# Ten of a group's 36 probability tiles turned through memory in place of seven, kept weights in 2 KB packets, new instruction orders

## The reference

```python
def attention(x):                       # on layernorm(x)
    q = rmsnorm((x @ Wq.T) per head, q_norm_w)      # 32 heads of 128
    k = rmsnorm((x @ Wk.T) per head, k_norm_w)      # 8 heads of 128
    v = x @ Wv.T                                    # 8 heads of 128
    scores = q @ k.T / sqrt(128)                    # 4 query heads share one k/v head
    bias = where(rel > 0, -1e30, slope[head] * rel) # causal, rel = key - query
    return (softmax(scores + bias) @ v) @ Wo.T
def lora(x):                            # on layernorm(x)
    gates = 8 * softmax(x @ Wr.T + br)              # 8 experts of rank 16
    return 2 * sum over h of gates[h] * (x @ A[h].T) @ B[h].T
x = x + attention(layernorm(x)); x = x + lora(layernorm(x))
```

## Time and profile before

| | |
|---|---|
| median of 3 runs | 2136.99 us (2133.37 to 2137.82) |
| the profiled execution's own time | 2138.16 us |
| its span, first to last instruction | 2136.3 us |
| granted TensorE clock, mean | 0.993 |
| instructions | 33509 |
| busy share: PE, DVE, ACT, POOL | 98%, 63%, 54%, 44% |
| DMA | 329095 packets, 176.81 MB, of which 243800 packets under 512 bytes |

### The profile page before, as it was taken

One profiled execution on the slowest core, in us unless ns is written; L12 is line 12 of the kernel. 1 busy time (PEld: TensorE's weight loads), 2 busy tenths in 40 slices (PEclk: granted clock), 3 DMA queues, 4 the chain that ended last, 5 costly groups with the idle time before them and its releaser, 6 DMA issues.

```text
span 2136.3 us, 33509 instructions
## 1 busy us (share of the span) xinstructions
PE 2083.0 (98%) x11772; PEld 1786.4 (84%) x11772; DVE 1355.6 (63%) x3431; ACT 1148.2 (54%) x3314; POOL 936.1 (44%) x984
## 2 busy tenths in 40 slices
PE   7999999999999999999999999999999999999997
PEld 6888888888888888888888888888888888888885
DVE  6656656566565665658876556566566656656676
ACT  4555545555454654645445555555555555555552
POOL 3443434444444443444443544435453443545443
PEclk9999999999999999999999999999999999999998
DMA  4152141511415125051350422313041231304112
GB/s 158 64 140 75 30 130 64 154 60 40 133 54 150 60 55 157 16 154 55 110 157 7 113 70 68 101 50 92 28 107 62 67 102 50 89 30 106 44 36 73
DMA packets 329095, 176.81 MB, mean 83 GB/s; under 512 B 243800, under 2 KB 301144, under 8 KB 320736
## 3 DMA queue, kind: packets, MB, share of 16 engines
q1 hardware_dynamic: 305264, 72.41, 15.3%
q10 hardware_dynamic: 23664, 102.25, 12.8%
HBM read 99.11 MB, written 75.50 MB: 82 GB/s over the span
## 4 chain that ended last, share of the span: by engine, by line
PE 83%; DVE 4%; issue 4%; DMA 3%; SPq 2%; POOL 2%; ACT 2%; ACTq 0%; DVEq 0%; POOLq 0%
PE s_ps L1026 17%; PE q_ps L1026 15%; PE y_ps L1026 15%; PE o_ps L1026 15%; PE turn_ps L1113 13%; PE turn_ps L1026 5%; DMA p_raw<-p_bounce 3%; SPq L568 2%; POOL probs_odd L799 1%; PE turn_ps L1107 1%; PE y_ps L1186 1%; DVE pT_lo L898 1%; DMA p_bounce<-probs_odd 1%; DVE y L955 0%; DVE oT_lo L949 0%
## 5 line engine op out<-in xcount | busy, mean ns | idle before, releaser
L799 POOL TENSOR_TENSOR probs_odd<-probs_odd,p_inv 128x256 f32<-128x256 f32 (+3 forms) x256 | 316.4, 1256 | 326.9 <-DVE p_inv L928 326.9
L706 ACT ACTIVATE pT_hi<-turn_ps 128x512 fp32r<-128x512 f32 x464 | 271.6, 597 | 316.2 <-PE turn_ps L1113 315.9
L799 POOL TENSOR_TENSOR probs_even<-probs_even,p_inv 128x128 f32<-128x128 f32 (+3 forms) x256 | 261.8, 1044 | 386.1 <-DVE p_inv L928 386.1
L898 DVE TENSOR_TENSOR pT_lo<-turn_ps,pT_hi 128x512 fp32r<-128x512 f32 x464 | 314.6, 684 | 146.2 <-ACT pT_hi L706 145.2
L921 DVE CUSTOM_DVE_ANT_0 probs_odd<-s_ps,rel 128x256 f32<-128x256 f32 (+3 forms) x256 | 209.3, 820 | 131.9 <-issue 131.4
L1026 PE MATMUL s_ps<-kT_hi,qT_hi 128*128 128x512 f32 (+3 forms) x768 | 278.7, 363 | 2.6 <-DVE kT_lo L900 1.8
L1026 PE MATMUL s_ps<-kT_hi,qT_lo 128*128 128x512 f32 (+3 forms) x768 | 262.9, 342 | 0.0
L1026 PE MATMUL s_ps<-kT_lo,qT_hi 128*128 128x512 f32 (+3 forms) x768 | 262.1, 341 | 0.0
L720 ACT ACTIVATE probs_odd<-probs_odd,neg_max 128x256 f32<-128x256 f32 (+3 forms) x256 | 211.9, 832 | 76.0 <-DVE neg_max L921 75.9
L921 DVE CUSTOM_DVE_ANT_0 probs_even<-s_ps,rel 128x128 f32<-128x128 f32 (+3 forms) x256 | 174.0, 686 | 118.0 <-issue 117.2
L1026 PE MATMUL o_ps<-pT_hi,v_hi 128*128 128x512 f32 x576 | 243.9, 423 | 1.9 <-DVE pT_lo L898 0.9
(11 more groups left out here) (110 smaller groups left out, 4578.6 us busy)
## 6 DMA issues: line engine op xcount, KB each, us to landing
p_raw<-p_bounce SPq DMA_DIRECT2D x448, 64.0 KB, 2.3
p_bounce<-probs_odd SPq DMA_DIRECT2D x64, 256.0 KB, 2.3
wq_kept<-wqT_hi ACTq DMA_DIRECT2D x8, 1024.0 KB, 5.8
wq_kept<-wqT_lo ACTq DMA_DIRECT2D x8, 1024.0 KB, 8.4
wo_kept<-woT_hi ACTq DMA_DIRECT2D x8, 1024.0 KB, 8.1
wo_kept<-woT_lo ACTq DMA_DIRECT2D x8, 1024.0 KB, 10.2
p_bounce<-probs_even SPq DMA_DIRECT2D x64, 128.0 KB, 1.8
wqT_hi<-wq_kept ACTq DMA_DIRECT2D x8, 1024.0 KB, 4.8
```

The costliest lines, as they stand in the source:

```text
L706: nc.scalar.activation(target, bank, ACT.Copy).then_inc(sems["high"], 1)
L799: nc.gpsimd.tensor_tensor(row, row, p_inv[:, s % 2, h:h + 1].to_broadcast((P, L)), ALU.mult).then_inc(sems["normalise"], 1)
L898: nc.vector.tensor_tensor(target, bank, upper.bitcast(F32), ALU.subtract).then_inc(sems["low"], 1)
```

## The change

Three things are edited. The table gets three more tiles: (4,4), (5,4) and (6,4), so 10 of 36 go through memory. The kept weights get another layout in HBM, with one piece of 512 floats for each partition after the other, so that a packet has 2 KB where it had 4 KB (wkv) or 8 KB (wq, wo). And all the lists are written anew; GROUP_A is shown in part.

```diff
-MEMORY_TILES = {5: (5,), 6: (5, 6), 7: (4, 5, 6, 7)}
+MEMORY_TILES = {4: (4,), 5: (4, 5), 6: (4, 5, 6), 7: (4, 5, 6, 7)}
 GROUP_A = (
...
-    "high.p.6.0 o_low.5 fetch_p.6.5 high.p.6.1 low.p.6.0 exp.7.2 low.p.6.1 send_p.7.1 fetch_p.6.6 scores.7.3 "
...
+    "fetch_p.6.4 square_q.8 low.p.6.0 load_wkv y.5 inv_q.8 max.7.2 exp.7.1 high.p.6.1 invert.7.0 normalise.7.0 "
+    "exp.7.2 scores.7.3 low.p.6.1 values.6.0 max.7.3 normalise.7.1 send_p.7.0 values.6.1 fetch_p.6.5 turn.p.6.2 "
+    "add_y.5 exp.7.3 turn.kv.0 norm_q.8 high.p.6.2 fetch_p.6.6 invert.7.1 flip_p.6.4 normalise.7.2 low.p.6.2 "
+    "upper_p.6.4 send_p.7.1 turn.p.6.3 high.kv.0 normalise.7.3 send_p.7.2 turn.kv.1 keep_wq low.kv.0 high.p.6.3 "
+    "lower_p.6.4 send_p.7.3 low.p.6.3 flip_p.6.5 values.6.2 flip_p.6.6 upper_p.6.5 values.6.3 high.kv.1 lower_p.6.5 "
+    "values.6.4 fetch_p.7.4 low.kv.1 q.9.0 upper_p.6.6 turn.p.7.0 lower_p.6.6 q.9.1 fetch_p.7.5 high.p.7.0 turn.q.8 "
+    "low.p.7.0 values.6.5 high.q.8 values.6.6 fetch_p.7.6 low.q.8 turn.p.7.1 o_high.6 turn.kv.2 load_wo o_low.6 "
+    "high.p.7.1 flip_p.7.4 low.p.7.1 upper_p.7.4 lower_p.7.4 values.7.0 high.kv.2 values.7.1 fetch_p.7.7 low.kv.2 "
...
-        wkv_kept = nc.dram_tensor("wkv_kept", [NG, 2, P, C * 2 * HD], F32).ap()
-        wq_kept = nc.dram_tensor("wq_kept", [NG, 2, P, C * W512], F32).ap()
-        wo_kept = nc.dram_tensor("wo_kept", [NG, 2, P, G * DM], F32).ap()
+        wkv_kept = nc.dram_tensor("wkv_kept", [NG, 2, C // 2, P, W512], F32).ap()
+        wq_kept = nc.dram_tensor("wq_kept", [NG, 2, C, P, W512], F32).ap()
+        wo_kept = nc.dram_tensor("wo_kept", [NG, 2, G, P, DM], F32).ap()
+
+        def pieces(kept, g, part):
+            return kept[g, part].rearrange("c p n -> p c n")
+
+        def pairs(turned):
+            return turned[:].rearrange("p (a c) n -> p a (c n)", c=2).bitcast(F32)
...
-                act.dma_start(wq_kept[w + 1, 0], wqT_hi[:].rearrange("p c n -> p (c n)").bitcast(F32)).then_inc(wq_spilled, 16)
+                act.dma_start(pieces(wq_kept, w + 1, 0), wqT_hi[:].bitcast(F32)).then_inc(wq_spilled, 16)
...
-                act.dma_start(wqT_hi[:].rearrange("p c n -> p (c n)").bitcast(F32), wq_kept[g, 0]).then_inc(wq_back, 16)
+                act.dma_start(wqT_hi[:].bitcast(F32), pieces(wq_kept, g, 0)).then_inc(wq_back, 16)
```

More of the change, by code:

```diff
@@ L630, in keep_wkv @@
                 after(act, "low", "wkv", w + 1, 1)
-                act.dma_start(wkv_kept[w + 1, 0], wkvT_hi[:].rearrange("p c n -> p (c n)").bitcast(F32)).then_inc(wkv_spilled, 16)
-                act.dma_start(wkv_kept[w + 1, 1], wkvT_lo[:].rearrange("p c n -> p (c n)").bitcast(F32)).then_inc(wkv_spilled, 16)
+                act.dma_start(pieces(wkv_kept, w + 1, 0), pairs(wkvT_hi)).then_inc(wkv_spilled, 16)
+                act.dma_start(pieces(wkv_kept, w + 1, 1), pairs(wkvT_lo)).then_inc(wkv_spilled, 16)
             def keep_wq(w):
                 after(act, "low", "wq", w + 1, C - 1)
-                act.dma_start(wq_kept[w + 1, 0], wqT_hi[:].rearrange("p c n -> p (c n)").bitcast(F32)).then_inc(wq_spilled, 16)
-                act.dma_start(wq_kept[w + 1, 1], wqT_lo[:].rearrange("p c n -> p (c n)").bitcast(F32)).then_inc(wq_spilled, 16)
+                act.dma_start(pieces(wq_kept, w + 1, 0), wqT_hi[:].bitcast(F32)).then_inc(wq_spilled, 16)
+                act.dma_start(pieces(wq_kept, w + 1, 1), wqT_lo[:].bitcast(F32)).then_inc(wq_spilled, 16)
             def keep_wo(w):
                 after(act, "low", "wo", w, G - 1)
-                act.dma_start(wo_kept[w, 0], woT_hi[:].rearrange("p c n -> p (c n)").bitcast(F32)).then_inc(wo_spilled, 16)
-                act.dma_start(wo_kept[w, 1], woT_lo[:].rearrange("p c n -> p (c n)").bitcast(F32)).then_inc(wo_spilled, 16)
+                act.dma_start(pieces(wo_kept, w, 0), woT_hi[:].bitcast(F32)).then_inc(wo_spilled, 16)
+                act.dma_start(pieces(wo_kept, w, 1), woT_lo[:].bitcast(F32)).then_inc(wo_spilled, 16)
             def back_wkv(w):
@@ L647, in back_wkv @@
                 act.wait_ge(wkv_spilled, 32 * NG)
-                act.dma_start(wkvT_hi[:].rearrange("p c n -> p (c n)").bitcast(F32), wkv_kept[g, 0]).then_inc(wkv_back, 16)
-                act.dma_start(wkvT_lo[:].rearrange("p c n -> p (c n)").bitcast(F32), wkv_kept[g, 1]).then_inc(wkv_back, 16)
+                act.dma_start(pairs(wkvT_hi), pieces(wkv_kept, g, 0)).then_inc(wkv_back, 16)
+                act.dma_start(pairs(wkvT_lo), pieces(wkv_kept, g, 1)).then_inc(wkv_back, 16)
             def back_wq(w):
@@ L654, in back_wq @@
                 act.wait_ge(wq_spilled, 32 * NG)
-                act.dma_start(wqT_hi[:].rearrange("p c n -> p (c n)").bitcast(F32), wq_kept[g, 0]).then_inc(wq_back, 16)
-                act.dma_start(wqT_lo[:].rearrange("p c n -> p (c n)").bitcast(F32), wq_kept[g, 1]).then_inc(wq_back, 16)
+                act.dma_start(wqT_hi[:].bitcast(F32), pieces(wq_kept, g, 0)).then_inc(wq_back, 16)
+                act.dma_start(wqT_lo[:].bitcast(F32), pieces(wq_kept, g, 1)).then_inc(wq_back, 16)
             def back_wo(w):
@@ L661, in back_wo @@
                 act.wait_ge(wo_spilled, 32 * NG)
-                act.dma_start(woT_hi[:].rearrange("p c n -> p (c n)").bitcast(F32), wo_kept[g, 0]).then_inc(wo_back, 16)
-                act.dma_start(woT_lo[:].rearrange("p c n -> p (c n)").bitcast(F32), wo_kept[g, 1]).then_inc(wo_back, 16)
+                act.dma_start(woT_hi[:].bitcast(F32), pieces(wo_kept, g, 0)).then_inc(wo_back, 16)
+                act.dma_start(woT_lo[:].bitcast(F32), pieces(wo_kept, g, 1)).then_inc(wo_back, 16)
             def high(w, of, *which):
```

## The result

The changed kernel takes **2154.02 us** in the median of 4 runs (2153.06 to 2155.26), beside 2137.40 us for the kernel before on the same chip. The ratio is 1.0075, 95% interval 1.0062 to 1.0088: 0.75% slower, where the prediction had 1.5% faster. Its profiled execution took 2153.44 us, with a span of 2151.6 us and a mean granted clock of 0.989.

The account below looks back on a forecast made before the run. PE, busy 98%, was taken as the bound: 2138.2 - 20.6 - 16.6 + 7.0 - 6.8 + 3.2 + 2.0 = 2106.4 us profiled, 1.2 above the median of runs, so 2105 us predicted, range 2091 to 2122.

Parts of the forecast that it names:

- The turns: 48 tiles over 16 groups no longer turned by PE, at some 0.43 us a tile: 20.6 us off PE.
- So the wait at y goes: Groups 0 to 6: y's addition ahead of the last flips and transfers moved remove PE's seven y waits, 16.6 us gained.
- I take 1.0 us of wait in each of 7 groups: Value product 7.1 waits for its lower half behind the flip of 7.4: 7.0 us back.
- one for one: Packets of the two DMA queues pass about equally at either size, giving the fetch 3.5 times its rate beside kept weights.
- My bound of 2.9 us: Upper bound per group for the new wait at tile 7.1, today's longest; the lower bound was 0.
- The clock drops: Four falls to 1.2 GHz behind y waits of 1.9 to 2.95 us, none expected at 1.0: 6.8 us gained.
- 2 KB packets: Kept weights' smaller packets would free SP's issues; by the skill page's rule of whole bundles, the edit would be worth nothing.
- Short waits: New slips on PE, such as three s=6 tiles sharing two memory slots, 0.2 us a group: 3.2 us lost.
- The last group: Chain from tile 7's last normalising to product 7.7 has less PE work to hide it: 2.0 us lost, bounds 0 and 3.
- Two of the signs: Wrong if POOL lower-half waits exceed 0.5 us a group, flips wait 3 us with PE behind, or first-batch clock drops.
- the fetched tiles come too late: Slower rival: ten tiles, three raw buffers and POOL's work delay value products in all 16 groups, 2167 us; chance 0.04.

Follow-up runs that it names:

- e6: Kernel before, seven tiles and own lists, with only the keeping of wq moved behind the group's last upper_p in groups 0 to 6: 2109.48 us, ratio 0.9867.
- e1: Changed kernel with only the keeping of wq moved behind the last fetched tile's high half in groups 0 to 6: 2108.92 us, ratio 0.9868 to before.
- e13: Kernel before with only the addition of y for token tile 5 moved ahead of the flip of 7.5, groups 0 to 6: 2140.36 us, ratio 1.0009.
- e5: Changed kernel with both the keeping of wq and the load of Wo moved behind the last upper_p, groups 0 to 6: 2106.27 us, ratio 0.9854.
- e9: Changed kernel with wq's keeping and Wo's load late, but groups 7 and 15 with seven tiles and the lists of the kernel before: 2100.48 us, ratio 0.9827.
- e3: Changed kernel with the kept weights' old layout (8 KB pieces, wkv 4 KB), all lists and tiles as changed: 2151.86 us, ratio 1.0069 to before.
- e4: Kernel before with the kept weights' new layout alone (2 KB packets): 2140.58 us, ratio 1.0017.
- e8: Changed kernel with wq's keeping late, plus q.9.3 moved in groups 9 to 14 and token tile 6's gated-layer turns later in the last group: 2108.05 us.
- e11: Changed kernel with the keeping of wq moved earlier, directly behind low.wq.3 and beside that of wkv: 2108.22 us, ratio 0.9863 to before.
- e12: Changed kernel with only the lower half of wq (1 MB) kept late, behind the last upper_p: 2130.03 us, ratio 0.9971 to before.

## Why the prediction was wrong

The sum came to -31.8 us; the trace has +15.3. By stretches the 47 us are: groups 0 to 6 forecast -24.0, measured +9.6; group 7 -1.1 and +0.9; groups 8 to 14 -7.7 and -2.1; group 15 +0.9 and +6.2; ahead of group 0, 0 and +0.6.

- **The turns, -20.6 us: nearly right.** e6 against e1 gives 1.3 us for three tiles, 0.42 a tile as forecast, in groups 0 to 6, where nothing else stands. In the second batch PE's busy time falls by 1.1, 0.36 a tile, and the time by 0.2 to 0.3.
- **"So the wait at y goes", -16.6 us: right in the trace, wrong as a gain.** I took the place of the addition for the cause. e13 moved it alone and gained nothing; e6 left it alone, moved the transfer and gained 28 us, waits and clock drops together. The prediction had named the late fetch as the reason, and then booked the wait as if it hung on the order of DVE's queue.
- **"I take 1.0 us of wait in each of 7 groups": the step that failed.** The place was right, the size was 4.1 to 5.2 us, 31.8 us in all where 7.0 were booked. I counted wq's transfer against the fetch (3 us left of 5.4) and wrote that the send "adds a little since it too shares the engines". It is the send that falls into the transfer: 8.1 us to landing where e1 has 3.0. The load of Wo stands right ahead of the fetch, which I had noted in the list and not priced: 4.7 us to landing for 2.3. I had read the fetch beside that load as one for one, from 281.5 to 283.5 us of the kernel before. That stretch has wq's first packets in its second half; from 281.3 to 282.3, beside the load alone, 52 packets of the fetch pass while 135 of the load do. My bound of 2.9 us was the longest wait of the kernel before, and that is no bound for a chain in which three transfers now meet.
- **The clock drops, -6.8 us: wrong with it.** The waits of 4 us and more brought a low clock in every one of groups 0 to 6, in all 30.6 us at the lower level. Before it was 17: 13.6 in the four drops that the prediction counted and 3.4 at the head of group 0. At half of that time lost, as the prediction priced it, that is some 7 us more lost where 6.8 were to be gained. With the waits gone (e1, e5, e6, e9) there is none between 50 and 2070 us.
- **2 KB packets: nothing, as forecast.** e3 and e4 show no gain. SP's issues were not freed either: the longest of a fetch takes 2.9 us in e4 for 2.7 before. By the Trainium skill ("DMA: Bandwidth & Descriptors", Queues, rings and completion order) a bundle of descriptors passes before the engine turns to the other ring. That four small pieces then go as one large one was my own step; the page counts in descriptors. The counts of 348 to 332 at 2 KB and 99 to 61 at 8 KB fit single packets as well as equal bundles, and no run here shows a bundle.
- **Short waits, 3.2 us: too small.** In groups 9 to 14 it is 0.8 us each where 0.2 were booked: y.7 0.54 us behind the low half of o, and a value product 0.3 behind POOL's lower half. Each of the two is small; together they eat two thirds or more of what the three tiles give.
- **The last group, +2.0 us: too small.** With the turns and the short waits the forecast was +0.9, measured +6.2 (+5.4 and +7.3 between kernels with wq late, e5 and e1 against e6). e8 took away most of the wait for f_x and gained nothing, since others grew; what bounds this stretch stays open.

Two of the signs that the prediction had named against itself came: flips that wait 3 us and more for the DMA with PE behind them (5.41 in group 1), and clock drops in the first batch. The rival that came nearest is the slower one, "the fetched tiles come too late". It had the kind of wait and the drop of the clock behind it, but it expected POOL and the buffers as its cause, in all 16 groups. The cause was the sends under a transfer, in seven.

## What to carry to other kernels

Follow each bulk transfer to what is in flight beside it, the stores as well as the loads, and price the whole chain store, wait, fetch before a term for one part. When a wait on the bounding engine follows a late transfer, a new order on the engine between them may only move it, as in e13; try moving the transfer. And undo every independent part alone before crediting a change: here the move of one list item was worth 45 us in one kernel and 29 in the other, and all new tiles and lists together under 2, or 9 where they stayed out of two groups that they made longer (e9).

## What the runs showed that I had not expected

- The same 2 MB cost nothing under the first sends of token tile 6 (e11) or at the group's end (e1), and 45 us under the last sends of tile 7, halved with half the bytes (e12).
- A fetch of 64 KB pieces that was issued 1 us behind a load of 1 MB moved hardly a packet until that load was through. From 281 to 283 us of the changed kernel the DMA view has one queue only:

```profile
q10 hardware_dynamic: 266, 0.54, 91.0%
```

  That is not one for one, as the sends had it beside wq (318 to 288). Why a fetch from memory behind a load fares worse than a send beside a store was not tried.
- In e13 a wait of 1.6 to 2.55 us and one of 0.46 behind it were followed by the lower clock in five of seven groups; in the kernel before the single waits of 1.8 to 2.95 us were in four of seven, and not simply the longest four (2.46 us had none, 1.87 had one). The waits of 4.1 us and more of the changed kernel were in all seven.
